# All row scatters beside kernel 1, its softmax sums from a product with ones, and places and owners found by GpSimd in the inverse

## The chip, the cores and the metric

The kernel runs on one core of a Trainium2 chip, in one launch. TensorE (PE) multiplies, VectorE (DVE) and ScalarE (ACT) work on tiles, GpSimd (POOL) does the same and issues indirect DMAs, and SyncE (SP) issues plain DMAs. Each engine runs its own queue of instructions in order; semaphores tie them together. The metric is the device time of the whole launch in microseconds (us), lower being better. Before the change it is 2173.13 us, the median of three runs (2168.01 to 2175.15).

## The reference

Two transformer layers over 4096 rows of 256 numbers, in float32. Only the second concerns us. Its attention is a Nystrom attention (16 heads, 64 landmarks), and beside it stands a mixture of experts, both added to the input:

```python
kernel1 = softmax(einsum('bhnd,bhmd->bhnm', Q, K_l))       # rows against landmarks
kernel2 = softmax(einsum('bhmd,bhkd->bhmk', Q_l, K_l))     # landmarks against landmarks
kernel3 = softmax(einsum('bhmd,bhnd->bhmn', Q_l, K))
for _ in range(6):                                         # iterative_inv(kernel2)
    KV = K @ V
    V = 0.25 * V @ (13 * I - KV @ (15 * I - KV @ (7 * I - KV)))
SV = (kernel1 @ V) @ (kernel3 @ V_rows)
out = SV @ w_proj

scores = sigmoid(x @ router.T)                             # 16 experts, 4 chosen for each row
combine[row, expert] = 2.5 * score / (sum of the 4 chosen)
y = sum_e combine[:, e] * (silu(x @ gate_e.T) * (x @ up_e.T)) @ down_e.T + shared(x)
```

## The kernel before

The second layer runs as a row of stages. Each is an `nc.Block` in which every engine has its own program; the next stage begins when all engines have ended theirs. After kernel 3, whose DVE program also finds the rank of every expert for every row, come the three stages that matter here.

**`inverse` (line 1984).** The six iterations of the inverse for 32 matrices of 64x64, two stacked on the 128 partitions, in four groups `g`. PE computes a step for all four groups (64 pairs of weight load and matmul a step, 21 steps in all), DVE turns each result into the next factor (`polynomial`, `complement`), ACT copies others from PSUM. Beside it the routing is ended. Each row is sent to four slots in HBM, one for each of its four experts; `place[:, k]` holds the slot of a row's choice k, `share[:, k]` its weight, `owner` the expert of each tile of 128 slots. Choice 0 comes from kernel 3. DVE finds the choices 1 to 3 and the owners behind its own work of iterations 0 to 4 (`find_place_and_share`, `compare_owners`, `find_owners`, recorded at line 57 since they go through `Lanes`). SP loads the rows, 4 MB, into `x_rows`. POOL makes small constants and then issues the first 64 (`EARLY`) of 128 scatters: each writes 128 rows of 272 numbers from `x_rows` to their slots. One set of 32 scatters stands for one choice k; before the next set the tag columns of `x_rows` are rewritten, for which the earlier scatters must have landed (lines 2046 to 2057).

**`kernel1` (line 2193).** 32 tiles of 128 rows, in a software pipeline: `staggered(engine, N, DEPTH, [(lag, body), ...])` writes out turns 0 to N + DEPTH, and in turn i each body works on tile i - lag, in the order of the list. For a tile: PE multiplies rows by landmarks (`scores`, into `k_p`), DVE takes the maximum and subtracts it (`shift`), ACT exponentiates (`exp`, `k_e`), DVE sums and takes the reciprocal (`sums`, `k_rs`), POOL multiplies (`normalise`, `k_en`), PE transposes (`turn`, `k_pt`), ACT copies (`take_turned`), PE multiplies by the landmarks' values (`values`, `k_pv`), ACT copies (`take_values`), PE multiplies by w_proj (`output`, `k_po`), DVE adds x1 (`add`, into `QT`). POOL issues two of the remaining 64 scatters ahead of each `normalise`. SP loads the experts' weights first (`load_ahead`) and then the tiles of x1 (`k_x`).

**`experts` (line 2397).** 72 steps of two tiles of slots: load, gate and up, down, and a scatter back to `s_parts`; then the shared experts and the sum. The change does not touch it.

## Time and profile before

| | us |
|---|---|
| median of three runs | 2173.13 |
| the profiled execution | 2178.65 |
| its span in the trace | 2176.2 |
| PE busy in the span | 1814.4 (83%) |
| DVE busy | 1514.0 (70%) |
| ACT busy | 1031.5 (47%) |
| POOL busy | 536.8 (25%) |

The trace covers the span; 2.45 us of the profiled execution lie around it. Busy time is an average over stages with different limits, so the rows further down are read stage by stage. "Idle before" is the idle time of an engine just ahead of an instruction, with what ended it; "issue" stands where the profile shows nothing that was waited for. PE's matmuls and weight loads overlap and have rows of their own (PE and PEld). DMA-issuing instructions of POOL are shown with the time for which they occupy it.

### The profile page before, as it was taken

How to read it: one execution, taken by the hardware profiler on the slowest of the kernel's cores; microseconds unless marked ns; L12 is line 12 of the kernel's file. 1: busy time of each engine (PE TensorE's matmuls, PEld its weight loads, DVE VectorE, ACT ScalarE, POOL GpSimd, SP SyncE). 2: the span in 40 equal slices, each digit the busy share in tenths (PEclk: the TensorE clock that was granted, in tenths of full speed). 3: DMA queues.
4: the chain of work that ended last, by engine and by line, in shares of the span. 5: the costliest groups of instructions: out<-in, count | busy, mean ns of one | idle time of the engine just before them, and what ended most of it. 6: DMA issues, size and time to landing. Idle time of an engine off the chain costs nothing. (4 is left out here: it accounts for less than half of the span.)

```text
span 2176.2 us, 34165 instructions
## 1 busy us (share of the span) xinstructions
PE 1814.4 (83%) x11999; PEld 944.1 (43%) x11999; DVE 1514.0 (70%) x3496; ACT 1031.5 (47%) x1908; POOL 536.8 (25%) x592
## 2 busy tenths in 40 slices
PE   0898926899999999999899959799327788999998
PEld 0565602222222222222223236555317555888865
DVE  7987656888888888888788845378206896444456
ACT  3554403466667666666566825356001444323210
POOL 1443350000000000000340000100650786566620
PEclk9999958999999999999999989999658899999999
DMA  3466563013030404040620163000420622566556
GB/s 97 140 212 220 187 157 69 1 25 127 12 140 3 148 2 150 2 150 2 227 79 11 40 230 128 18 2 1 158 85 9 214 95 94 175 188 187 185 198 222
DMA packets 158712, 238.67 MB, mean 110 GB/s; under 512 B 19762, under 2 KB 127282, under 8 KB 156882
## 3 DMA queue, kind: packets, MB, share of 16 engines
q1 hardware_dynamic: 122706, 152.46, 23.0%
q0 software_dynamic: 23136, 75.65, 9.5%
q10 hardware_dynamic: 12704, 8.39, 1.2%
q8 instruction: 99, 1.62, 0.3%
q14 instruction: 67, 0.55, 0.1%
HBM read 116.23 MB, written 119.82 MB: 108 GB/s over the span
## 5 line engine op out<-in xcount | busy, mean ns | idle before, releaser
L1051 ACT ACTIVATE c_prob<-c_pst 128x512 f32<-128x512 f32 (+1 forms) x1152 | 603.1, 573 | 362.3 <-PE c_pst L1012 221.5
L1159 DVE TENSOR_REDUCE c_mx<-c_pf 128x2 f32<-128x1024 f32 x384 | 463.0, 1223 | 92.3 <-PE c_pf L993 89.4
L1012 PE MATMUL c_pst<-c_qa,c_ka 128*128 128x512 bf16 (+3 forms) x1280 | 393.9, 358 | 38.2 <-DMA c_qa<-c_mT 34.6
L993 PE MATMUL c_pf<-c_ka,c_qa 64*128 64x512 bf16 (+3 forms) x1280 | 234.9, 364 | 79.2 <-DVE c_mx L1159 26.4
L1028 PE MATMUL c_po<-c_prob,c_vh 128*32 128x512 f32 (+3 forms) x2560 | 297.2, 547 | 1.5 <-DVE c_osb L1187 0.5
L1155 DVE CUSTOM_DVE_ANT_0 c_spare<-c_pf,c_cut 128x384 f32<-128x384 f32 (+3 forms) x512 | 231.1, 492 | 51.0 <-PE c_pf L993 46.3
L1012 PEld LDWEIGHTS c_pst<-c_qa,c_ka 128*128 128x128 bf16 x1280 | 108.6, 97 | 284.4 <-ACT c_prob L1051 122.7
L993 PEld LDWEIGHTS c_pf<-c_ka,c_qa 64*128 64x128 bf16 x1280 | 61.9, 93 | 313.0 <-issue 126.5
L925 POOL IOTA c_zero<- 128x24 int32 x6 | 1.3, 215 | 697.4 <-PE c_po L1028 697.4
L1980 POOL DMA_INDIRECT s_parts<-x_yr,x_tags x144 | 141.0, 979 | 85.8 <-DVE x_yr L2635 62.4
L2519 PE MATMUL x_ps<-x_gu,x_xs 128*128 x576 | 137.6, 382 | 0.0
L1980 POOL DMA_INDIRECT s_slots<-x_rows,place x128 | 125.8, 983 | 37.9 <-issue 31.3
L2620 DVE TENSOR_TENSOR x_h<-x_ps,x_sg 128x256 f32<-128x256 f32 x72 | 30.6, 424 | 142.4 <-ACT x_sg L2589 123.5
L2067 PE MATMUL i_pm<-i_X,i_AQ 64*64 64x64 f32 x768 | 41.9, 248 | 82.7 <-issue 70.3
L2519 PEld LDWEIGHTS x_ps<-x_gu,x_xs 128*128 128x128 f32 x576 | 105.0, 192 | 11.5
L1016 PE MATMUL c_pst<-c_negk,c_idb 128*128 128x128 bf16 x512 | 95.7, 220 | 0.0
L1028 PEld LDWEIGHTS c_po<-c_prob,c_vh 128*32 128x32 f32 x2560 | 54.6, 109 | 86.4 <-issue 43.2
L2582 ACT COPY x_xs<-x_ps 128x512 f32<-128x512 f32 x72 | 42.2, 587 | 84.5 <-issue 61.3
L2067 PEld LDWEIGHTS i_pm<-i_X,i_AQ 64*64 64x64 f32 x768 | 35.9, 159 | 88.3 <-issue 75.2
L2540 PE MATMUL x_ps<-x_d,x_hT 128*128 x288 | 74.1, 380 | 0.1
L365 POOL TENSOR_TENSOR b_parts<-b_r,b_parts 128x512 bf16<-128x512 f32 x32 | 57.6, 1819 | 57.7 <-ACT b_parts L502 57.7
L2335 ACT ACTIVATE k_e<-k_d 128x1024 f32<-128x1024 f32 x32 | 33.9, 1060 | 74.0 <-POOL k_en L2271 50.5
(383 smaller groups left out, 2934.9 us busy)
## 6 DMA issues: line engine op xcount, KB each, us to landing
s_slots<-c_zero POOLq DMA_DIRECT2D x6, 3264.0 KB, 19.9
x_xr<-s_slots SPq DMA_DIRECT2D x72, 272.0 KB
x_rows<-s_parts SPq DMA_DIRECT2D x8, 2048.0 KB, 8.8
c_qa<-s_qs SPq DMA_DIRECT2D x64, 192.0 KB, 8.3
c_ka<-s_ks SPq DMA_DIRECT2D x64, 192.0 KB, 9.0
s_qs<-b_parts SPq DMA_DIRECT2D x32, 256.0 KB, 2.4
s_ks<-b_parts SPq DMA_DIRECT2D x32, 256.0 KB, 2.7
s_vs<-b_va SPq DMA_DIRECT2D x32, 256.0 KB, 3.8
```

Source lines behind the costliest of these rows:

```text
L365: nc.gpsimd.tensor_tensor(parts[:, i, 2, :], r[:, i, :], parts[:, i, 1, :], ALU.subtract).then_inc(parts_ok, 1)
L993: mm = nc.tensor.matmul(pf[:, slot, h - fh, 0:kn], qa[r, s, h, qt * P:(qt + 1) * P], ka[r, s, h, k0:k0 + kn], start=True, stop=True, tile_ ...
L1012: mm = nc.tensor.matmul(pst[:, u % NS, at:at + qn], ka[:, s, hh, kt * P:(kt + 1) * P], qa[:, s, hh, qb * QB + q0:qb * QB + q0 + qn], start ...
L1016: mm = nc.tensor.matmul(pst[:, u % NS, at:at + P], idb[:], negk[:], start=False, stop=True)
L1028: mm = nc.tensor.matmul(po[HV * h:HV * h + HV, q0:q0 + qn], vh[:, s, kt, h, :], prob[:, a % NP, h, at:at + qn], start=(kt == 0), stop=(a i ...
L1051: nc.scalar.activation(prob[:, g % NP, hh, 0:w], pst[:, u % NS, 0:w], ACT.Exp).then_inc(exp_ok, 1)
L1155: ins = nc.vector.tensor_tensor_reduce(spare[:, h, 0:kn], pf[:, slot, h, 0:kn], cut[:, W1 - kn:], 1.0, 0.0, ALU.add, ALU.max, mx[:, fh + h ...
L1159: nc.vector.tensor_reduce(mx[:, fh:fh + 2, qt, part], pf[:, slot, :, 0:kn], AX.X, ALU.max).then_inc(max_ok, 1)
L1980: return nc.gpsimd.indirect_dma_start(out=dst, out_offset=bass.IndirectOffsetOnAxis(ap=index.bitcast(U32), axis=0), in_=src, in_offset=None)
L2067: mm = nc.tensor.matmul(out[h, s % 2 * NG + g, k, 0:width], lhs(h, n), rhs(h, n), start=True, stop=True, tile_position=(h.start, h.start))
L2519: mm = nc.tensor.matmul(pgu[:, m % 2, i, :], xs[:, m % 2, i, k, :], gu[:, k, bass.ds(e, 1), :].rearrange("p o n -> p (o n)"), start=(k == ...
L2540: mm = nc.tensor.matmul(pyr[:, m % 2, i, :], hT[:, m % 2, i, :], d[:, bass.ds(e, 1), :].rearrange("p o n -> p (o n)"), start=True, stop=True)
```

## The change

The 64 early scatters leave `inverse`. In their place POOL finds places and shares of the choices 1 to 3 and the owners, in steps that each wait for the one before; a sum over the 16 experts is made by adding halves (8, 4, 2, 1). DVE's program in `inverse` loses that work. POOL waits for the load of `x_rows` at the stage's end.

In `kernel1` POOL issues all 128 scatters, four for each tile, and does nothing else after its constants. `k_e` is transposed as it is, not normalised. PE multiplies the transposed tile not only by the values but also by a matrix of ones (`ones`, block-diagonal, 128x32), which gives each head's sum, repeated on the 16 partitions of that head, beside its values in `k_pv`. DVE takes the reciprocal of these sums (128x256 from PSUM) and multiplies the values by it (`divide`), which replaces `sums` on DVE, `normalise` on POOL and `take_values` on ACT. The pipeline is shorter (DEPTH 6 for 8) and its bodies are ordered anew.

```diff
-            nc.gpsimd.tensor_copy(tiles_f[:], tiles_i[:]).then_inc(consts, 1)
-            nc.gpsimd.memset(xrows[:, :, C:], 0.0).then_inc(tag_ok, 1)
-            pool.wait_ge(tag_ok, 1)
-            for k in range(-(-early // NR)):
-                if k:
-                    pool.wait_ge(sent, 16 * k * NR)
-                nc.gpsimd.iota(xrows[:].bitcast(I32)[:, :, C:C + 1], pattern=[[P * TOPK, NR], [1, 1]], base=k,
-                               channel_multiplier=TOPK).then_inc(tag_ok, 1)
-                wait(pool, share_ok, k)
-                nc.gpsimd.tensor_copy(xrows[:, :, C + 1:C + 2], share[:, k].unsqueeze(2)).then_inc(tag_ok, 1)
-                pool.wait_ge(tag_ok, 2 * k + 3)
-                for t in range(min(NR, early - k * NR)):
-                    if k == 0 and t in (0, NR // 4):
-                        pool.wait_ge(rows_in[t // (NR // 4)], 16)
-                    scatter(nc, slots_dram, place[:, k, t:t + 1], xrows[:, t, :]).then_inc(sent, 16)
-            pool.wait_ge(sent, 16 * early)
+            step(nc.gpsimd.tensor_copy(tiles_f[:], tiles_i[:]))
+            step(nc.gpsimd.memset(xrows[:, :, C:], 0.0))
+            def sum_experts(dst, terms):
+                for n in (8, 4, 2):
+                    step(nc.gpsimd.tensor_tensor(terms[:, :, 0:n], terms[:, :, 0:n], terms[:, :, n:2 * n], ALU.add))
+                step(nc.gpsimd.tensor_tensor(dst, terms[:, :, 0], terms[:, :, 1], ALU.add))
+            def of_choice(dst, val, k):
+                step(nc.gpsimd.tensor_scalar(by[:], rank[:, 0], float(k), None, ALU.is_equal))
+                step(nc.gpsimd.tensor_tensor(by[:], by[:], val, ALU.mult))
+                sum_experts(dst, by)
+            for k in range(1, TOPK):
+                of_choice(placef[:], ahead[:].rearrange("p e t -> p t e"), k)
+                step(nc.gpsimd.tensor_copy(place[:, k], placef[:]))
+                of_choice(share[:, k], comb[:], k)
+            step(nc.gpsimd.tensor_tensor(before[:], ends[0:1, :].unsqueeze(1).to_broadcast([1, NT, E]), over(tiles_f[:], E), ALU.subtract))
+            step(nc.gpsimd.tensor_scalar(before[:], before[:], 0.0, None, ALU.is_le))
+            sum_experts(tiles_f[:], before)
+            step(nc.gpsimd.tensor_scalar(tiles_f[:], tiles_f[:], float(E - 1), None, ALU.min))
+            step(nc.gpsimd.tensor_copy(owner[:], tiles_f[:]))
+            for i in range(2):
+                pool.wait_ge(rows_in[i], 16)
...
-                both(nc.vector.scalar_tensor_tensor, by[:], rank[:, 0], float(k), val, ALU.is_equal, ALU.mult)
-                both(nc.vector.tensor_reduce, dst, by[:], AX.X, ALU.add)
-            def find_place_and_share(k):
-                of_choice(placef[:], ahead[:].rearrange("p e t -> p t e"), k)
-                both(nc.vector.tensor_copy, place[:, k], placef[:])
-                of_choice(share[:, k], comb[:], k)
...
-            def compare_owners():
-                dve.wait_ge(consts, 1)
-                both(tt, before[:], ends[0:1, :].unsqueeze(1).to_broadcast([1, NT, E]), over(tiles_f[:], E), ALU.is_le)
...
-                both(nc.vector.tensor_reduce, ownerf[:], before[:], AX.X, ALU.add)
-                both(ts, ownerf[:], ownerf[:], float(E - 1), None, ALU.min)
-                both(nc.vector.tensor_copy, owner[:], ownerf[:])
...
                 if it < LAST:
                     complement(it + 1)
-                if it + 1 < TOPK:
-                    find_place_and_share(it + 1)
-                elif it + 1 == TOPK:
-                    compare_owners()
-                elif it == TOPK:
-                    find_owners()
...
-    N, DEPTH = B * NT, 8
+    N, DEPTH = B * NT, 6
...
-    en = sb("k_en", [P, 2, H, M])
+    ones = sb("k_ones", [P, 2 * D])
     et = sb("k_et", [P, 2, H // 2, P])
-    mx, sm, rs = (sb(f"k_{n}", [P, 2, H]) for n in ("mx", "sm", "rs"))
+    mx = sb("k_mx", [P, 2, H])
+    rs = sb("k_rs", [P, K, P])
...
-    pv = ps("k_pv", [P, K, P])
+    pv = ps("k_pv", [P, 2, K, P])
...
-            staggered(sp, N, DEPTH, [(6, load)])
+            staggered(sp, N, DEPTH, [(4, load)])
...
+            step(nc.gpsimd.memset(ones[:], 0.0))
+            for h in range(2):
+                step(nc.gpsimd.memset(ones[h * M:(h + 1) * M, h * D:(h + 1) * D], 1.0))
...
-            per = -(-(TOPK * NR - early) // N)
+            per = TOPK * NR // N
 
             def send(n, u, s):
-                for i in range(early + n * per, min(early + n * per + per, TOPK * NR)):
-                    k, t = i // NR, i % NR
-                    if t == 0:
-                        wait(pool, sent, 16 * (i - early))
-                        nc.gpsimd.iota(xrows[:].bitcast(I32)[:, :, C:C + 1], pattern=[[P * TOPK, NR], [1, 1]], base=k,
-                                       channel_multiplier=TOPK).then_inc(tag_ok, 1)
-                        nc.gpsimd.tensor_copy(xrows[:, :, C + 1:C + 2], share[:, k].unsqueeze(2)).then_inc(tag_ok, 1)
-                        pool.wait_ge(tag_ok, 2 * (k - early // NR + (early % NR == 0)))
+                k, t0 = divmod(n * per, NR)
+                if t0 == 0:
+                    wait(pool, sent, 16 * NR * k)
+                    nc.gpsimd.iota(xrows[:].bitcast(I32)[:, :, C:C + 1], pattern=[[P * TOPK, NR], [1, 1]], base=k,
+                                   channel_multiplier=TOPK).then_inc(tag_ok, 1)
+                    nc.gpsimd.tensor_copy(xrows[:, :, C + 1:C + 2], share[:, k].unsqueeze(2)).then_inc(tag_ok, 1)
+                    pool.wait_ge(tag_ok, 2 * (k + 1))
+                for t in range(t0, t0 + per):
                     scatter(nc, slots_dram, place[:, k, t:t + 1], xrows[:, t, :]).then_inc(sent, 16)
 
-            def normalise(n, u, s):
-                wait(pool, r_ok, n + 1)
-                wait(pool, t_ok, n - 1)
-                nc.gpsimd.tensor_tensor(en[:, s], e[:, s], over(rs[:, s], M), ALU.mult).then_inc(n_ok, 1)
-            staggered(pool, N, DEPTH, [(0, send), (3, normalise)])
-            wait(pool, sent, 16 * (TOPK * NR - early))
+            staggered(pool, N, 0, [(0, send)])
+            wait(pool, sent, 16 * TOPK * NR)
 
...
             def turn(n, u, s):
-                wait(pe, n_ok, n + 1)
+                wait(pe, e_ok, n + 1)
 
                 wait(pe, ta_ok, n)
                 for i in range(H // 2):
-                    mm = nc.tensor.transpose(pt[:, i, :], en[:, s, 2 * i:2 * i + 2, :].rearrange("p h m -> p (h m)"), ident[:])
+                    mm = nc.tensor.transpose(pt[:, i, :], e[:, s, 2 * i:2 * i + 2, :].rearrange("p h m -> p (h m)"), ident[:])
...
                 wait(pe, va_ok, n)
                 for k in range(K):
                     for g in range(4):
-                        mm = nc.tensor.matmul(pv[32 * g:32 * g + 32, k, :], W[:, s * (H // 2) + k * 4 + g, :],
-                                              et[:, s, g // 2 * 4 + k * 2 + g % 2, :],
+                        nc.tensor.matmul(pv[32 * g:32 * g + 32, 0, k, :], W[:, s * (H // 2) + k * 4 + g, :],
+                                         et[:, s, g // 2 * 4 + k * 2 + g % 2, :],
+                                         start=True, stop=True, tile_position=(0, 32 * g))
+                    for g in range(4):
+                        mm = nc.tensor.matmul(pv[32 * g:32 * g + 32, 1, k, :], ones[:], et[:, s, g // 2 * 4 + k * 2 + g % 2, :],
                                               start=True, stop=True, tile_position=(0, 32 * g))
                 mm.then_inc(v_ok, 1)
...
-            staggered(pe, N, DEPTH, [(5, turn), (1, scores), (6, output), (5, values)])
+            staggered(pe, N, DEPTH, [(1, scores), (3, turn), (4, output), (3, values)])
...
             def exp(n, u, s):
                 wait(act, d_ok, n + 1)
 
-                wait(act, n_ok, n - 1)
+                wait(act, t_ok, n - 1)
                 nc.scalar.activation(e[:, s], d[:, s], ACT.Exp).then_inc(e_ok, 1)
 
-            def take_values(n, u, s):
-                wait(act, v_ok, n + 1)
-                wait(act, o_ok, n - 1)
-                nc.scalar.copy(svt[:, s], pv[:]).then_inc(va_ok, 1)
-            staggered(act, N, DEPTH, [(5, take_turned), (2, exp), (5, take_values)])
+            staggered(act, N, DEPTH, [(3, take_turned), (2, exp)])
...
-            def sums(n, u, s):
-                wait(dve, e_ok, n + 1)
-                nc.vector.tensor_reduce(sm[:, s], e[:, s], AX.X, ALU.add).then_inc(sum_ok, 1)
-                wait(dve, sum_ok, n + 1)
-                wait(dve, n_ok, n - 1)
-                nc.vector.reciprocal(rs[:, s], sm[:, s]).then_inc(r_ok, 1)
+            def divide(n, u, s):
+                wait(dve, v_ok, n + 1)
+                nc.vector.reciprocal(rs[:], pv[:, 1]).then_inc(rs_ok, 1)
+                wait(dve, rs_ok, n + 1)
+                wait(dve, o_ok, n - 1)
+                nc.vector.tensor_tensor(svt[:, s], pv[:, 0], rs[:], ALU.mult).then_inc(va_ok, 1)
...
-            staggered(dve, N, DEPTH, [(7, add), (2, shift), (3, sums)])
+            staggered(dve, N, DEPTH, [(4, divide), (5, add), (2, shift)])
```

## Rows read from the trace of the kernel before

**Rows 1.** Busy time of each engine (instructions), PEclk, DMA share, GB/s, by stretch.
```profile
1529.30:1541.00 11.70, 8.00 (x252) 7.64 (x252) 5.18 (x13) 1.86 (x5) 7.07 (x15) 1.00 0.90 298
1541.00:1626.00 85.00, 14.81 (x75) 9.88 (x75) 5.44 (x10) 1.12 (x3) 59.16 (x63) 0.52 0.31 114
1626.00:1683.60 57.60, 44.96 (x1017) 44.30 (x1017) 34.13 (x72) 11.51 (x24) 0.00 (x0) 0.85 0.01 2
1683.60:1840.20 156.60, 126.61 (x1152) 86.81 (x1152) 133.78 (x164) 72.76 (x96) 126.55 (x105) 0.93 0.39 132
1840.20:2176.20 336.00, 321.68 (x1552) 255.80 (x1552) 157.56 (x280) 80.79 (x161) 155.51 (x218) 0.98 0.60 192
```
**Rows 2.** Waits, 1529 to 1683: engine and line, releaser: total us, times, longest.
```profile
PE i_pm L2067 <- issue: 73.3, 49, 2.7
PE i_pm L2067 <- DVE i_X L2163: 11.6, 4, 3.4
```
**Rows 3.** Timeline of PE, 1535.9 to 1541.4: start, us, instruction [idle before <-releaser].
```profile
1539.11 1.73 PE L2067 MATMUL i_pm<-i_AQ 64*64 64x64 f32 x52 [2.67 <-issue]
```
**Rows 4.** Timeline of PE, 1619 to 1627.
```profile
1621.37 0.26 PE L2067 MATMUL i_pm<-i_X,i_AQ 64*64 64x64 f32 x1 [2.54 <-issue]
...
1624.88 0.36 PE L2067 MATMUL i_pm<-i_X,i_AQ 64*64 64x64 f32 x1 [0.44 <-issue]
```
**Rows 5.** DMA queues, 1529.3 to 1626: packets, MB, share of 16 engines.
```profile
q8 instruction: 3, 0.05, 0.2%
```
**Rows 6.** Lines, 1541 to 1626: busy us, mean ns | idle before, releaser.
```profile
L1980 POOL DMA_INDIRECT s_slots<-x_rows,place x61 | 59.4, 974 | 18.6 <-issue 18.6
```
**Rows 7.** Timeline of PE, one step of the inverse.
```profile
1670.35 2.08 PE L2067 MATMUL i_pm<-i_X,i_AQ 64*64 64x64 f32 x64
```
**Rows 8.** The page's costliest groups: POOL's operations with two inputs.
```profile
L2271 POOL TENSOR_TENSOR k_en<-k_e,k_rs 128x1024 f32<-128x1024 f32 x32 | 61.1, 1912 | 7.2 <-DVE k_rs L2366 6.6
L365 POOL TENSOR_TENSOR b_parts<-b_r,b_parts 128x512 bf16<-128x512 f32 x32 | 57.6, 1819 | 57.7 <-ACT b_parts L502 57.7
```
**Rows 9.** Timeline of POOL at the change from choice 0 to choice 1.
```profile
1576.19 0.96 POOL L1980 DMA_INDIRECT s_slots<-x_rows,place  x1 [0.31 <-issue]
...
1579.41 1.01 POOL L1980 DMA_INDIRECT s_slots<-x_rows,place  x1 [0.28 <-issue]
```
**Rows 10.** Timeline of DVE, one turn of kernel 1.
```profile
1718.61 0.36 DVE L2373 TENSOR_TENSOR QT<-k_po,k_x 128x256 f32<-128x256 f32 x1
1718.91 1.23 DVE L2354 TENSOR_REDUCE k_mx<-k_p 128x16 f32<-128x1024 f32 x1
1720.17 1.23 DVE L2358 TENSOR_TENSOR k_d<-k_p,k_mx 128x1024 f32<-128x1024 f32 x1
1721.31 1.21 DVE L2362 TENSOR_REDUCE k_sm<-k_e 128x16 f32<-128x1024 f32 x1
```
**Rows 11.** Groups of DVE's instructions by form, whole span.
```profile
L1202 DVE TENSOR_TENSOR c_att<-c_pf,c_rec 128x256 f32<-128x256 f32 x32 | 13.6, 424 | 1.3 <-DVE c_rec L1197 0.3
...
L2366 DVE RECIPROCAL k_rs<-k_sm 128x16 f32<-128x16 f32 x32 | 8.1, 253 | 1.1
...
L1472 DVE RECIPROCAL d_nq<-d_rc 128x4 f32<-128x4 f32 x8 | 1.4, 178 | 0.3
```
**Rows 12.** Timeline of PE, one turn of kernel 1.
```profile
1721.37 0.64 PE L2308 MATMUL k_pv<-k_et,W 128*32 128x128 f32 x16
1721.94 1.09 PE L2299 MATMUL k_pt<-k_ident,k_en 128*128 128x128 f32 x8
1722.97 1.13 PE L2288 MATMUL k_p<-k_kbd,QT 64*128 64x256 f32 x8
1724.03 1.13 PE L2318 MATMUL k_po<-k_wp,k_svt 128*128 128x256 f32 x4
```
**Rows 13.** Timeline of DVE: the first tile's add.
```profile
1714.47 0.42 DVE L2373 TENSOR_TENSOR QT<-k_po,k_x 128x256 f32<-128x256 f32 x1 [7.34 <-DMA k_x<-s_x]
```
**Rows 14.** Lines, 1855.4 to 2086, the experts' scatters.
```profile
L1980 POOL DMA_INDIRECT s_parts<-x_yr,x_tags x144 | 141.0, 979 | 85.8 <-DVE x_yr L2635 62.4 <-issue 23.4
```

More of the change, by code:

```diff
@@ L1981, in scatter, with inverse @@
                                         in_offset=None)
-def inverse(nc, KTb, Vb, VTb, tbd, W, comb, rank, ends, ahead, place, share, owner, rows_dram, xrows, slots_dram, early, TOPK, NPR, ITERS,
+def inverse(nc, KTb, Vb, VTb, tbd, W, comb, rank, ends, ahead, place, share, owner, rows_dram, xrows, TOPK, NPR, ITERS,
             ctx):
@@ L2003, in inverse @@
     C = xrows.shape[2] - 16
-    chain = sem("r_chain2")
     tiles_i = sb("r_tiles_i", [1, NT], I32)
@@ L2009, in inverse @@
     before = sb("r_before", [1, NT, E])
-    ownerf = sb("r_ownerf", [1, NT])
-    consts, share_ok, tag_ok, sent = (sem(f"r_{n}") for n in ("consts2", "share_ok", "tag_ok", "sent"))
     chain_p = sem("r_chain_p")
@@ L2125, in _ @@
             dve.wait_ge(eye_ok, 3)
-            lanes = Lanes(dve, chain, 2)
-            tt, ts = nc.vector.tensor_tensor, nc.vector.tensor_scalar
-            def both(operation, *operands):
-                lanes.join(1)
-                lanes(0, operation, *operands)
-                lanes.last[1] = lanes.last[0]
-            def of_choice(dst, val, k):
-                both(nc.vector.scalar_tensor_tensor, by[:], rank[:, 0], float(k), val, ALU.is_equal, ALU.mult)
-                both(nc.vector.tensor_reduce, dst, by[:], AX.X, ALU.add)
-            def find_place_and_share(k):
-                of_choice(placef[:], ahead[:].rearrange("p e t -> p t e"), k)
-                both(nc.vector.tensor_copy, place[:, k], placef[:])
-                of_choice(share[:, k], comb[:], k)
-                lanes.join(0)
-                dve.sem_inc(share_ok, 1)
-            def compare_owners():
-                dve.wait_ge(consts, 1)
-                both(tt, before[:], ends[0:1, :].unsqueeze(1).to_broadcast([1, NT, E]), over(tiles_f[:], E), ALU.is_le)
-            def find_owners():
-                both(nc.vector.tensor_reduce, ownerf[:], before[:], AX.X, ALU.add)
-                both(ts, ownerf[:], ownerf[:], float(E - 1), None, ALU.min)
-                both(nc.vector.tensor_copy, owner[:], ownerf[:])
-                lanes.join(0)
             def polynomial(s, dst, e, scale):
@@ L2217, in kernel1 @@
     pt = ps("k_pt", [P, H // 2, P])
[L2218 removed]
+    pv = ps("k_pv", [P, 2, K, P])
     po = ps("k_po", [P, 512])
[L2220 to L2221 removed]
+    id0, id_ok, hm_ok, w_in, kbd_ok, chain_p, max_ok, rs_ok = (
+        sem(f"k_{n}") for n in ("id0", "id_ok", "hm_ok", "w_in", "kbd_ok", "chain_p", "max_ok", "rs_ok"))
     tag_ok, sent = sem("k_tag_ok"), sem("k_sent")
     TOPK, NR = place.shape[1], place.shape[2]
[L2224 to L2225 removed]
+    s_ok, d_ok, e_ok, t_ok, ta_ok, v_ok, va_ok, o_ok, x2_ok = (
+        sem(f"k_{n}") for n in ("s_ok", "d_ok", "e_ok", "t_ok", "ta_ok", "v_ok", "va_ok", "o_ok", "x2_ok"))
     x_in = [sem(f"k_x_in{i}") for i in range(2)]
@@ L2718, in two_layers @@
                 owner = layer.enter_context(nc.sbuf_tensor("owner", [1, NSLOT], I32))
-                EARLY = 64
                 with ExitStack() as lm:
@@ L2748, in two_layers @@
                         with ExitStack() as c:
-                            inverse(nc, *stacked, tbd, W, comb, rank, ends, slots_ahead, place, share, owner, rows_dram, xrows, slots, EARLY, TOP_K, NPR, ITERS, c)
+                            inverse(nc, *stacked, tbd, W, comb, rank, ends, slots_ahead, place, share, owner, rows_dram, xrows, TOP_K, NPR, ITERS, c)
                     gu, d, w_in, load = expert_weights(nc, gate_w, up_w, down_w, sh_gate_w, sh_up_w, sh_down_w, C, I, E, NSH, lm)
                     with ExitStack() as c:
-                        kernel1(nc, QT, KS, W, w_proj, x1, load, place, share, xrows, slots, EARLY, B, T, C, M, DA, c)
+                        kernel1(nc, QT, KS, W, w_proj, x1, load, place, share, xrows, slots, B, T, C, M, DA, c)
                     with ExitStack() as c:
```

6 lines of the change are left out of this document (1 added, 5 removed).

## The prediction

> **What bounds the kernel now.** I read the stages around the change first [rows 1]. The inverse (1529.3 to 1683.6, 154.3 us) falls into three parts. In the first 11.7 us PE issues 252 weight-and-matmul pairs. In the next 85.0 us it issues 75, at PEclk 0.52, while POOL issues scatters. In the last 57.6 us it issues 1017. Kernel 1 takes 156.6 us with DVE busy 133.8, PE 126.6 and POOL 126.6; the experts take 336.0 us with PE busy 321.7, and nothing in them is touched.
>
> Next, who waits in the inverse [rows 2]: PE idles 73.3 us on "issue", that is, on nothing that the profile shows, and 11.6 us on DVE's `i_X`. The DVE operations queued ahead of that `i_X` are the places, shares and owners that the change moves away. The timeline shows the "issue" idle to be one event. PE halts at 1536.4, 2.67 us ahead of the row at 1539.11, resumes there with 52 pairs in 1.73 us [rows 3], and then crawls with gaps as long as 2.54 us [rows 4] until it runs freely from 1626 on. From the halt to the free run it issues 52 + 75 = 127 pairs [rows 1, 3], 254 instructions; the queue that carries code moved 3 packets of 16 KB in this time [rows 5]. So the halt looks like a wait for code: it begins while the 4 MB load of `x_rows` holds the DMA engines 90% busy, and the crawl lies over the run of scatters, 1.28 us apart (59.4 + 18.6 us for 61) [rows 6].
> The Trainium skill ("Runtime: NRT & Kernel Launch", Instruction fetch mechanics) says that code comes in blocks of 256 instructions, fetched ahead and mostly hidden. The block size fits the 254; that the fetch is hidden is not what these rows show.
>
> What counts is thus PE's stall in the inverse, and in kernel 1 the longest of three nearly equal loops.
>
> **The inverse.** Removed: 64 scatters. I take the crawl to go with them and the halt to stay, since the `x_rows` load stays. PE has 21 groups of 64 pairs, 1344. After 1541.0, 1344 - 252 = 1092 remain. The last 1017 took 57.6 us, of which 11.6 were the DVE waits [rows 1, 2], hence 46.0; the 75 that crawled cost 75 x 2.08/64 = 2.4 us [rows 7]. The inverse ends at 1541.0 + 46.0 + 2.4 = 1589.4, 94.2 us earlier. Bounds: a new short wait for code adds up to another 2.7 us; less time at half clock takes some 4 away.
>
> Added on POOL: six times an is_equal over 512 elements, a product over 512, adds over 256, 128, 64 and 32, and three casts; then the owners, about 2304 x 2 + 2160 elements on one partition. POOL's two-input operation costs 1.91 us for 1024 elements (1.87 ns each) in one row and 1.82 us for 512 (3.55 ns each) in another [rows 8]. With the first, nearest in type, a choice is 1504 x 1.87 ns = 2.8 us and some 0.8 us of gaps, so 22 us for six, and the owners 6768 x 1.87 ns = 12.7 us and gaps: 36 us, ended near 1569 and covered by PE's stage. With the second it is 39 + 25 = 64 us, ended near 1597, 8 us past PE. I take the first and keep the 8 us.
>
> **Kernel 1, POOL.** Removed: 32 x 1.91 us of `k_en` [rows 8]. Added: 64 scatters. Its queue is now only setup, about 3 us, 128 x 1.28 = 163.8 us, three changes of rank that cost 1.9 us each (1576.19 + 1.28 to 1579.41) [rows 9], and 2 us until the last lands: 175 us. This is a floor under kernel 1 however fast the rest is, 18 us above today's 156.6.
>
> **Kernel 1, DVE.** Removed: the sum of `k_e`, 1.21 us, and the reciprocal of 16, 0.25 us. Kept, from start to start: the add 0.30, the maximum 1.26, the difference 1.14 us [rows 10]. Added: a product 128x256 from PSUM, 0.42 us as `c_att`, and a reciprocal 128x256. No row has that size. From 4 to 16 elements the time rises from 0.178 to 0.253 us, 6.3 ns an element [rows 11], so 256 cost 0.253 + 240 x 0.0063 = 1.76 us; the lower bound is any other 256-wide operation, 0.42 us. I take 1.76, from the rows of the same operation. One turn is 1.76 + 0.42 + 0.30 + 1.26 + 1.14 = 4.9 us, and a few tenths of semaphores: 5.05 us, against the 1.46 + 2.70 = 4.2 us of now.
> The Trainium skill ("VectorE: DVE Perf Modes", First, the fixed hardware budget) describes reciprocal as an iterated divide with a repeat count of 8 at 0.96 GHz; as an estimate from that page 256 elements would be 2.1 us and the turn 5.4. The slope in the rows is lower, and the sum goes by it.
>
> **Kernel 1, PE.** The turned values, transposes, scores and output take 0.57 + 1.03 + 1.06 + 1.13 us from start to start [rows 12]; the 16 passes with ones add about 0.6: 4.4 us, up to 5.0 with today's issue gaps. The transposes need not wait for POOL any more. A chain also closes over both engines: reciprocal and product 2.2, output 1.13, values and ones 1.2, semaphores 0.3, near 4.9. So DVE, PE and the chain stand close to each other, DVE a little ahead.
>
> The first add waits for `k_x`, queued on SP behind the expert weights, until 30.9 us after the stage's start [rows 13]; that queue is unchanged, so the wait stays, and shift and divide are queued behind it on DVE. After it: 2.8 us of that turn, 28 turns x 5.05 = 141.4, and the drain of three short turns, 9.5. Kernel 1 takes 30.9 + 2.8 + 141.4 + 9.5 + 0.4 = 185.0 us, 28.4 more than now; bounds 175 (POOL's floor, if the reciprocal is cheap) and 200 (turn 5.5). ACT loses its copy of the values and idles more, worth nothing.
>
> **Sum.** 2176.2 - 94.2 + 28.4 = 2110.4 us of span, with the 2.45 us around it 2112.9 against the profiled run's 2178.65: 65.8 us less. The median, 2173.13, lies 5.5 below that run, so I forecast 2107.
>
> **Rivals.**
> *The crawl moves into kernel 1.* There 128 scatters now run back to back as in the inverse, the expert weights load over the first 30 us, and PE has 52 pairs a tile where it had 36. If PE runs out of code there once, it pays the same block: 85 us. Against it: kernel 1 and the experts have scatters now (the experts one per 1.6 us [rows 14]) and PE issues freely in both; it needs 104 instructions in 5.05 us, 21 per us; the inverse needed 128 in 2.08 us [rows 7], 62 per us. It decides when code arrives later than one block's 12 us. Price: 2107 + 85 = 2192, slower. Chance 0.10.
> *The crawl is the load's, not the scatters'.* The halt at 1536.4 precedes nearly all scatters; if a late block stays slow whatever POOL does, the inverse keeps its 85 us, loses 11.6 of DVE waits, and kernel 1 still grows by 28.4: 2173.1 - 11.6 + 28.4 = 2190, slower. For it: 254 instructions are as much a block as they are the run of scatters. Against: the crawl's gaps fall from 2.54 us to 0.44 by 1624.88, within 6 us of the last scatters [rows 4], and no other saturated load in the trace brings one. Chance 0.09.
> *POOL is the bound.* Either the reciprocal is cheap, and kernel 1 is 175 us: 2097, inside the forecast; or POOL's vector work is dear and the inverse ends 8 us later: 2115. Both are in the main case.
> *The scatters only shorten the crawl's part.* A second late block, or a partial crawl of 20 to 60 us: 2127 to 2167, faster still or the same. Chance 0.07.
>
> **Chances.** Main case 0.74, own range 2088 to 2135 (bounds of reciprocal, POOL work and code waits: -10, +15, +8, +3 and some slack). Extended by the partial crawls, 2085 to 2150 holds eight in ten. A measurement of this kernel tells about 0.3%, 6.5 us, from no change. Faster: 0.74 and most of 0.07, 0.80; same 0.02; slower 0.18.
>
> **What would show it.** The inverse: PE's "issue" idle falls from 73.3 to under 10 us, PEclk stays near 1, the stage lasts about 60 us. POOL's vector work there sums to 30 to 40 us and ends before PE. Kernel 1: POOL shows 128 scatters 1.28 us apart and nothing else; the reciprocal's mean is 1.7 us; DVE's turn 5.0 us; the stage lasts 175 to 200 us. Wrong would be: long "issue" idle of PE in either stage; a reciprocal near 0.4 us (then POOL ends last); DVE busy under 120 us in kernel 1; or experts that change their 336 us.

## The result, and the profile after

The changed kernel took 2259.93 us (median of 4 runs, 2254.83 to 2268.75) beside 2170.57 us for the kernel before (4 runs, 2167.47 to 2175.15): a ratio of 1.0414, interval 1.0373 to 1.0455. It is slower by 4%; the forecast was 2107 us.

Later runs add a second result. The experiments ran on five chips, and these behaved in two ways. On chips 2 and 13 the kernel before took 2171.4 and 2174.1 us (one run each), as here. On chips 5, 9 and 11 it took 2111 to 2128 us (27 runs). On chip 9 the changed kernel took 2106.89 us (9 runs) beside 2116.33 (18 runs): a ratio of 0.9939, interval 0.992 to 0.9957. I call the first sort of chip "held" and the second "free"; the runs below show why. The held runs all came before the free ones, and no chip was used in both, so whether it is the chip or something at that time isn't shown.

The stages of the changed kernel in its profiled run (2257.39 us, span 2255.7): the inverse, the first kernel, the experts. Columns: stretch, length, busy time and count of PE, PEld, DVE, ACT, POOL, granted clock, DMA share, GB/s.
```profile
1526.80:1585.80 59.00, 48.19 (x1344) 47.04 (x1344) 39.16 (x76) 14.46 (x32) 49.10 (x56) 1.00 0.23 74
1585.80:1920.10 334.30, 152.03 (x1664) 104.20 (x1664) 156.73 (x164) 65.99 (x64) 127.59 (x144) 0.73 0.25 89
1920.10:2255.70 335.60, 321.60 (x1552) 255.77 (x1552) 157.33 (x280) 80.58 (x161) 155.17 (x218) 0.98 0.60 192
```
Against [rows 1], the inverse fell from 154.3 to 59.0 us (60.1 forecast). The experts are unchanged (336.0, 335.6). The first kernel rose from 156.6 to 334.3 us (185.0 forecast). All of the miss, 149 us, is in that stage, where no engine is busy for half of the time.

Who waits there, from the waits of 1585.8 to 1920 (us in total, times, longest):
```profile
ACT k_et L2299 <- remote: 167.3, 2, 99.0
DVE k_rs L2326 <- remote: 165.0, 2, 132.6
...
POOL s_slots L1980 <- issue: 41.0, 125, 3.3
...
PE k_pv L2275 <- issue: 35.7, 2, 34.5
```
ACT and DVE wait 165 us in a few long events on "remote", a releaser that the profile doesn't show; PE waits on "issue". PE's idle on "issue" in the inverse [rows 2, 3] had the same name. The timelines of PE, PEld, DVE and ACT (start, duration, work, idle time before):
```profile
1598.07 1.06 ACT L2305 ACTIVATE k_e<-k_d 128x1024 f32<-128x1024 f32 x1
1667.42 1.01 ACT L2299 COPY k_et<-k_pt 128x1024 f32<-128x1024 f32 x1 [68.29 <-remote]
1668.48 0.66 PE L2275 MATMUL k_pv<-k_et,W 128*32 128x128 f32 x8 [34.54 <-issue]
...
1680.00 0.37 PE L2279 MATMUL k_pv<-k_et,k_ones 128*32 128x128 f32 x1 [2.43 <-issue]
...
1716.40 0.37 PE L2266 MATMUL k_pt<-k_ident,k_e 128*128 128x128 f32 x1 [2.43 <-issue]
1717.80 0.18 PEld L2266 LDWEIGHTS k_pt<-k_ident,k_e 128*128 128x128 f32 x1 [2.62 <-issue]
...
1724.80 0.37 PE L2266 MATMUL k_pt<-k_ident,k_e 128*128 128x128 f32 x1 [2.43 <-issue]
...
1766.82 1.76 DVE L2326 RECIPROCAL k_rs<-k_pv 128x256 f32<-128x256 f32 x1 [132.62 <-remote]
...
1768.37 1.01 ACT L2299 COPY k_et<-k_pt 128x1024 f32<-128x1024 f32 x1 [98.98 <-remote]
```
Two things can be told apart. From 1673 to 1725 PE issues one weight load or matmul each 1.40 us. And DVE and ACT go on long after what they need has been issued: DVE's reciprocal at 1766.8 needs the product whose last matmul started at 1680.0, ACT's copy at 1667.4 the transposes of which the last started at 1605.8, ACT's copy at 1768.4 those of which the last started at 1724.8. PE's long idles follow from this lateness: the one of 34.54 us ends just behind ACT's copy of 1667.4, for which PE's program waits there, although the profile puts it down to "issue". From 1766.8 on the stage runs at a tile in 4.9 us. The scatters on POOL (durations, first and last start):
```profile
L1980 POOL DMA_INDIRECT s_slots<-x_rows,place x128: 956/969/1215, 1588.7 to 1759.4; - x128
```
The stall, which I call the crawl as in the inverse, begins some 12 us after the first scatter and ends 7 us after the last one starts. In the kernel before, the last of the inverse's scatters starts at 1619.0, and its crawl ends at 1626. Crawl and scatters moved together.

### The profile page after: what moved, and what is told of

The parts are those of the page before. It is cut to its first block and busy times, and to the rows that moved or that the text cites. A ratio compares the mean times of both kernels' runs of the same rounds, so it can differ in the third digit from the quotient of the medians.

```text
span 2255.7 us, 35074 instructions
## 1 busy us (share of the span) xinstructions
PE 1821.9 (81%) x12511; PEld 947.3 (42%) x12511; DVE 1530.4 (68%) x3477; ACT 1023.9 (45%) x1876; POOL 519.6 (23%) x610
## 5 line engine op out<-in xcount | busy, mean ns | idle before, releaser
L2326 DVE RECIPROCAL k_rs<-k_pv 128x256 f32<-128x256 f32 x32 | 56.3, 1758 | 169.1 <-remote 165.0
L2584 DVE TENSOR_TENSOR x_h<-x_ps,x_sg 128x256 f32<-128x256 f32 x72 | 30.6, 425 | 142.3 <-ACT x_sg L2553 112.1
L2299 ACT COPY k_et<-k_pt 128x1024 f32<-128x1024 f32 x32 | 32.4, 1012 | 204.8 <-remote 167.3
L2483 PEld LDWEIGHTS x_ps<-x_gu,x_xs 128*128 128x128 f32 x576 | 104.9, 192 | 11.6
L2288 PE MATMUL k_po<-k_wp,k_svt 128*128 128x256 f32 x128 | 38.0, 423 | 84.0 <-DVE QT L2337 58.4
```

The costliest lines, as they stand in the source:

```text
L2326: nc.vector.reciprocal(rs[:], pv[:, 1]).then_inc(rs_ok, 1)
L2483: mm = nc.tensor.matmul(pgu[:, m % 2, i, :], xs[:, m % 2, i, k, :], gu[:, k, bass.ds(e, 1), :].rearrange("p o n -> p (o n)"), start=(k == ...
```

## The experiments

Theory A: a dense run of scatters holds TensorE back. Theory B: a late block of code crawls whatever GpSimd does. Unless said otherwise, edits are to the changed kernel's `kernel1`.

**e1, the scatters last** (chip 2).
```
+            pool.wait_ge(x2_ok, N)
             staggered(pool, N, 0, [(0, send)])
```


> POOL waits until all 32 tiles of kernel 1 are added and only then issues the 128 scatters; all else as in the changed kernel. Theory A (a run of scatters 1.27 us apart holds back what PE sends and receives, for as long as it lasts): PE shows no idle on issue above 2 us in kernel 1; the tiles take 185 us by the prediction's own sum (150 at least), then 166 us of scatters follow, so the whole takes about 2270 us, like the changed kernel, although nothing overlaps. Theory B (a code block that comes late crawls, whatever POOL does): the long issue idle stays somewhere in kernel 1 and the whole takes 2350 us or more.


Measured: 2272.02 us. The tiles are done when the scatters begin at 1761.2, some 178 us after the stage began, and DVE's reciprocal waits 8.5 us in all, none of it "remote":
```profile
L2327 DVE RECIPROCAL k_rs<-k_pv 128x256 f32<-128x256 f32 x32 | 56.2, 1758 | 8.5 <-PE k_pv L2280 8.5
```
The same code without scatters beside it doesn't crawl. Theory B fails for this stage. Doing tiles and scatters in turn costs only 15 us more than doing them together (2257.4), so beside each other they gained almost nothing.

**e2 and e3, at most two or four scatters in flight** (chip 2).
```
+                    done, one = divmod(k * NR + t, 2)
+                    wait(pool, sents[one], 16 * done)
-                    scatter(...).then_inc(sent, 16)
+                    scatter(...).then_inc(sents[one], 16)
```


> At most two scatters in flight (two semaphores in turn, each scatter waits for the last but one). Theory A in the form that it is a backlog of scatters in flight: the backlog cannot form, scatters come 1.3 to 1.5 us apart, PE runs freely, kernel 1 takes 185 to 195 us and the whole about 2105 to 2120 us. Theory A in the form that it is the density: at 1.4 us the stall stays in good part, 2180 us or more. Theory B: no change from 2258 us.

> The same with at most four in flight. If a backlog of more than four forms in the changed kernel, this removes it and gives about 2107 us. If never more than two or three are in flight there (one lands about 2.8 us after its issue), the limit does nothing: 2258 us, and the density alone decides.


Measured: 2210.98 us with two, 2247.45 with four. A limit of four hardly slows the scatters (1585.9 to 1762.3), and the stall stays (ACT's `k_et` waits 122.0 us on "remote"). A limit of two stretches them to 1594.4 to 1800.0, and part of the stall goes. So a backlog of more than four scatters isn't needed for the stall; the distance of the scatters looked like the cause.

**e4 and e7, a gap after each scatter** (chips 2 and 13): the same scatters and waits, with GpSimd kept busy for 0.54 us (a spare block of 128x512) or 0.22 us (128x128).
```
                     scatter(...).then_inc(sent, 16)
+                    step(nc.gpsimd.memset(pad[:], 0.0))
```


> POOL clears a 128x512 tile of its own (0.52 us, and the wait for it) after each scatter, nothing limits what is in flight. Theory A by density: scatters come 1.9 to 2.0 us apart, sparser than the experts' 1.6 us, so PE runs freely; POOL then sets the end, 128 x 1.95 = 250 us, and the whole takes 2106 + 250 - 185 = about 2170 us. Theory B: PE stalls for a block nevertheless, 2250 us.

> The changed kernel with a clear of a spare 128x128 block (by the 128x512 one's 0.54 us an estimated 0.2 us) after each scatter: a scatter every 1.5 us, between 1.42 (two in flight, partial stall, 2211.0 us) and 1.79 (no stall, 2165.3 us). Theory A1, the stall sets in at a sharp rate above 1.5 us: the first kernel is still disturbed, 2190 to 2210 us. Theory A2, it is gone by 1.5 us: scatters done after 128 x 1.5 = 192 us, the whole 2165.3 - 128 x 0.29 = about 2128 us.


Measured: 2165.34 and 2164.99 us, 92 us less than the changed kernel's 2257.39, by slowing GpSimd. The reciprocal's group with 0.54 us, then with 0.22 us:
```profile
L2328 DVE RECIPROCAL k_rs<-k_pv 128x256 f32<-128x256 f32 x32 | 56.3, 1758 | 22.4 <-PE k_pv L2281 22.2
```
```profile
L2328 DVE RECIPROCAL k_rs<-k_pv 128x256 f32<-128x256 f32 x32 | 56.2, 1757 | 74.5 <-remote 67.0 <-PE k_pv L2281 7.6
```
The mean distance of the scatters (from first to last start, over 127) and the "remote" wait of the reciprocal in us: 1.34 us (the changed kernel), 165.0; 1.39 (e3), 82.1 and 63.3 on "issue"; 1.54 (e7), 67.0; 1.62 (e2, uneven), 80.2; 1.87 (e4), none. The mean hides the pattern. In the changed kernel and e3 nearly all scatters are 1.3 us apart, in e7 1.5, in e4 1.8. In e2 most are 1.3 to 1.4 us apart, with pauses of up to 3.6 us between them, which may be why it is held as much as e7 at a larger mean; no run tested that by itself. Neither of my two guesses for e7 (2190 to 2210, or 2128) came true: part of the stall remains, but GpSimd is done 39 us earlier than in e4, and the two cancel. Even in e4 most tiles take 5.38 us, three distances of 1.79, and not 4.9.

**e5, the gap in the kernel before** (chip 13): the same line behind the 64 scatters of its inverse.


> The kernel before with one change: in the inverse GpSimd clears a spare 128x512 block (0.54 us in the run with gaps) after each of its 64 scatters, so that they go out some 1.8 us apart in place of 1.27. Theory A, a dense run of scatters holds TensorE back: the inverse's TensorE runs at its own pace, the stage is then as long as GpSimd needs, 64 x 1.8 = 115 us and some 8 to 12 us around them, 123 to 127 us in place of 154.3, and the whole 2171 - 29 = about 2142 us; no gap of many microseconds without a releaser on TensorE. Theory B, TensorE's late part crawls for a reason of its own: the inverse stays at 154 us and the kernel at 2171 us. The timed result also says whether the crawl that my forecast read as a wait for code was this one.


Measured: 2150.96 us, 23 less than its neighbour of before. The inverse and the first kernel (the inverse really lasts from 1525.7 to 1658.6, so the first stretch leaves out a little at each end):
```profile
1526.80:1656.30 129.50, 56.54 (x1316) 54.68 (x1311) 44.60 (x95) 13.67 (x32) 102.75 (x138) 0.71 0.29 103
1656.30:1812.90 156.60, 127.65 (x1152) 87.62 (x1152) 133.32 (x163) 72.85 (x96) 126.45 (x105) 0.92 0.39 132
```
No wait of PE on "issue" is left among the stage's longest; the largest is 15.2 us on `i_X`. The inverse is now 132.9 us, as long as 64 scatters at 1.8 us and 18 us around them, more than the 8 to 12 that I had put down. The crawl of [rows 2 to 4] was the same one: theory B falls there too.

**e6, small rows** (chip 13): 128 scatters of rows of 64 bytes beside the tiles, the real ones after them.
```
+            for i in range(128):
+                scatter(nc, spare, place[:, i // NR, i % NR:i % NR + 1], small[:]).then_inc(small_sent, 16)
+            wait(pool, small_sent, 16 * 128)
+            pool.wait_ge(x2_ok, N)
             staggered(pool, N, 0, [(0, send)])
```


> The changed kernel with its 128 scatters moved behind the tiles of the first kernel (as in the run with the scatters last, 2272.0 us), and in their old place beside the tiles 128 scatters of rows of 16 numbers (64 bytes) each into a spare table: the same number of instructions and descriptors at the same 1.27 us, one sixteenth or so of the bytes. It does more work than the reference asks for. If it is the bytes that hold TensorE back: tiles at 4.9 us, about 2272 us. If it is the number of instructions or descriptors: TensorE stands as in the changed kernel while they go out (128 x 1.27 = 163 us with almost no tile done), and the whole is about 2272 + 130 to 165 = 2400 to 2437 us. In between: a share of both.


Measured: 2431.27 us, the full stall:
```profile
L2334 DVE RECIPROCAL k_rs<-k_pv 128x256 f32<-128x256 f32 x32 | 56.2, 1757 | 168.9 <-remote 133.3 <-issue 31.6 <-PE k_pv L2287 4.1
```
The same kernel on a free chip (e16) took 2284.65 us, so the stall costs 146.6 us with rows of 64 bytes; with rows of 1 KB it is 149.7 (e14). The bytes don't matter here; what is left is the instructions or their 128 rows each.

**e8, shared and paced** (chip 13): the inverse of the kernel before with 32 of the scatters (and the 128x512 block after each), and in the new first kernel:
```
-            staggered(pool, N, 0, [(0, send)])
+            for i in range(32, TOPK * NR):
+                k, t = divmod(i, NR)
...
+                scatter(nc, slots_dram, place[:, k, t:t + 1], xrows[:, t, :]).then_inc(sent, 16)
+                step(nc.gpsimd.memset(pad[:], 0.0))
```


> The new first kernel, but the inverse of the kernel before (places, shares and owners on VectorE), which sends 32 of the 128 scatters; each of the 128 is followed by the clear of a spare 128x512 block. If density alone was what cost the time: the inverse takes 32 x 1.8 + 8 to 12 = 66 to 70 us, the first kernel 96 x 1.8 = 173 us of GpSimd against 32 turns of 4.9 to 5.3 and some 14 to start, 173 to 184 us; together 239 to 254 against 310.9 before, so 2171 - 57 to 72 = 2099 to 2114 us. If part of the loss comes from elsewhere (VectorE in the inverse, or the scatters' bytes even when paced), 2130 us or more.


Measured: 2136.53 us beside 2174.07. It is faster than both kernels on that chip, though 30 us above the middle of what I expected. The inverse runs from 1524.8 to 1603.3, 78.5 us and not 66 to 70. That isn't the crawl, since the same kernel on a free chip (e18) has 78.8; in both, the last 256 matmuls run at a granted clock of 0.55. The first kernel took 196 us and not 173 to 184; on the free chip it took 187, so some 9 us of it come only on the held chip, where most tiles take 5.4 us and not 4.9.

**e9 to e12** ran on chip 5, where the kernel before took 2118.33 us (7 runs). Their times can't be set against the runs above.

e9, plain transfers in place of the small scatters (`nc.gpsimd.dma_start(spare[i * P:i * P + P], small[:])`, then a 128x384 block):


> The run with small rows (2431.3 us) with one difference: the 128 transfers that GpSimd issues beside the tiles are ordinary ones (128 rows of 64 bytes to fixed addresses), not scatters by an index; a clear of a spare 128x384 block after each keeps them about as far apart (0.54 + 0.42 us and the engine's steps between, an estimated 1.25 us). The real scatters follow the tiles. It writes a spare table that the reference doesn't ask for. If any transfer issued from GpSimd at that rate holds TensorE back: about 2400 to 2430 us. If it takes a scatter by an index: tiles at 4.9 us, as in the run with the scatters last, about 2272 us.


Measured: 2279.62 us, no stall; on this chip that doesn't tell the two kinds of transfer apart, since on chip 11 small scatters cause none either (e16).

e10, the old division: the whole `kernel1` of before, with 128 scatters in it.


> The changed kernel with its second part undone: the first kernel as before (VectorE's row sums, GpSimd's product k_en, one a tile), but with all 128 scatters in it, four a tile; the inverse as in the changed kernel. Theory A, only the rate of the scatters counts: k_en of 1.91 us parts each four scatters from the next four, a tile takes 4 x 1.27 + 1.91 = 7.0 us of GpSimd, the first kernel 14 + 32 x 7.0 = 238 us with TensorE late but never for long, so 2171 - 95 + 81 = 2157 us, up to 2190 if TensorE still stands through each four. Theory C, the run of four is already enough for a full stall: the first kernel as in the changed one, 320 us or more, 2245 us or more. Either way the second part of the change is priced by the distance to 2260 us.


Measured: 2160.86 us. The first kernel:
```profile
1585.80:1823.20 237.40, 149.18 (x1210) 102.29 (x1207) 137.70 (x164) 74.10 (x100) 188.60 (x173) 0.83 0.36 125
```
The stage itself runs from 1588.2 to 1824.4, so 2.4 us of the stretch belong to the inverse: 236.2 us for 238 expected, bound by POOL. The second part of the change is thus worth 51 us beside all scatters on a free chip (184.9 us there, e14). Whether a run of four is already enough for the stall, which this run was to tell, stays open: on a held chip it wasn't run.

e11, places and owners back on VectorE, with the gaps of e4.


> The run with gaps (2165.3 us) with the third part of the change undone: places, shares and owners are found by VectorE between its steps of the inverse, GpSimd has nothing in the inverse but its constants. If TensorE bounds the inverse either way: 59 us and 2165 us, within 3 us. If VectorE's extra work lies on the inverse's chain (its steps wait for each other): the inverse 62 to 70 us, 2168 to 2176 us. If GpSimd's 50 us were what kept the inverse at 59: below 2162 us.


Measured: 2174.93 us. The inverse lasts 72.5 us (1523.2 to 1595.7), against 62.3 in e4 and 59.0 in the changed kernel: the third part is worth 10 to 13 us of the inverse, near the 11.6 us of DVE waits that I took from [rows 2]. The setting differs from e4 in the chip too.

e12, e8 with 24 early scatters in place of 32.


> The shared and paced version (2136.5 us, inverse 75, first kernel 200) with 24 of the scatters in the inverse in place of 32, in three rounds. GpSimd is done with the inverse 8 x 1.79 = 14 us earlier, near 1576, so TensorE ends it near 1590 (63 to 66 us); then 14 us and 32 tiles of 5.4 us, 186 to 190 us, so the experts begin at about 1778 to 1786 and the whole is 2115 to 2123 us, a ratio of 0.974 to 0.978 to the kernel before. If the inverse's TensorE is still held back after the last scatter, 2128 us or more.


Measured: 2142.61 us, ratio 1.0127 (1.0094 to 1.0159): slower by 1.3%. The expected times and ratio took 2171 for the kernel before. Here GpSimd ends last (the tiles are done at 1778, the last scatter starts at 1793.7, and PE's `x_ps` waits 30.6 us for `x_xr`), and a tile beside scatters 1.79 us apart takes 4.87 us, not the 5.38 of e4.

**e13 to e16** put the question to one chip, 11, which proved to be of the free sort.


> The kernel before, unchanged, with its trace. Theory D, chips differ in how far a scatter holds TensorE back: where this takes about 2118 us, the inverse takes some 50 us less than 154.3 (95 to 110 us) and everything else is as it was; where it takes 2171, the inverse is 154 us again. Rival: the 53 us lie elsewhere (the attention or the experts), and the inverse is 154 us on both.

> The changed kernel, unchanged, with its trace. Theory D: on a chip where the kernel before takes 2118 us, the first kernel's scatters hold TensorE back by less, as the inverse's do: if the 64 scatters of the inverse cost some 40 us and not 94, 128 beside tiles cost 80 to 100 of the 165, so 2160 to 2190 us; if they cost next to nothing beside tiles, the forecast's 2107 us. On a chip where the kernel before takes 2171 us: 2255 to 2269 us again.

> The run with plain transfers again (2279.6 us, tiles 4.87 us apart, no stall). If a scatter by an index is what it takes: tiles at 4.9 us on any chip, 2272 to 2282 us. If the earlier run was undisturbed only for its chip, and this one is a chip of the other sort: 2350 us or more.

> The run with small scatters again (2431.3 us, TensorE standing through them), on the same chip as the plain transfers. If the scatter by an index is what it takes: on a chip where the kernel before takes 2171 us, 2425 to 2440 us again; where it takes 2118 us, more than the plain transfers by the share of the stall that chip has, 2300 to 2390 us. If the two kinds of transfer do the same: equal times, within 10 us.


Measured: 2115.92, 2107.71, 2274.02 and 2284.65 us. The kernel before (PE's part of the inverse from 1526.8 on, the rest of it, the first kernel, the experts; the inverse begins at 1521.2 here, so its first 149 matmuls are ahead of the stretch):
```profile
1526.80:1593.20 66.40, 48.51 (x1195) 47.61 (x1191) 41.59 (x87) 12.73 (x27) 48.79 (x50) 0.90 0.40 144
1593.20:1620.60 27.40, 0.04 (x2) 0.00 (x0) 0.00 (x0) 0.27 (x1) 16.00 (x17) 0.52 0.24 88
1620.60:1777.20 156.60, 127.64 (x1152) 87.82 (x1152) 133.76 (x164) 72.60 (x96) 126.72 (x106) 0.93 0.39 132
1777.20:2113.20 336.00, 322.00 (x1552) 255.99 (x1552) 157.58 (x280) 80.71 (x161) 155.26 (x217) 0.98 0.60 192
```
The changed kernel (the inverse, the first kernel, the experts):
```profile
1526.80:1585.80 59.00, 48.41 (x1344) 47.20 (x1344) 39.50 (x76) 14.49 (x32) 49.00 (x56) 1.00 0.22 74
1585.80:1770.20 184.40, 141.62 (x1664) 100.03 (x1664) 156.42 (x163) 66.10 (x64) 128.02 (x144) 0.94 0.47 161
1770.20:2106.00 335.80, 321.22 (x1552) 255.49 (x1552) 157.67 (x281) 80.75 (x161) 155.70 (x218) 0.98 0.60 192
```
Same kernels, scatters as dense as before (in the changed kernel from 1588.9 to 1762.2), and PE isn't held. The kernel before saves 63 us against its first profile: 54 in the inverse, which lasts 100.1 us here (1521.2 to 1621.3) for 154.3, and 8 ahead of it, where the start of the inverse differs by up to 12 us from run to run (1519.5 to 1531.1). The changed kernel saves 150, all in the first kernel. Without the crawl the old inverse is bound by GpSimd's 64 scatters: PE is done at 1593.2, 28 us ahead of the stage's end. The change then takes 41 us from the inverse (100.1 to 59.2) and gives the first kernel 29 (155.6 to 184.9), 12 us less by stages. These two profiles differ by only 7 us of span, since the inverse begins 5.7 us later in the changed kernel's; the nine runs of e17 tell 9 us. Small scatters and plain transfers both leave PE alone here, so e9 and e15 don't tell whether plain transfers stall PE on a held chip. That wasn't tried on one.

**e17 and e18**, on chip 9, of the free sort: the changed kernel (9 runs) and e8's (10 runs).


> The changed kernel, unchanged, in rounds beside the kernel before. On a chip where the kernel before takes 2112 to 2121 us: 2104 to 2112 us, a ratio of 0.994 to 0.999, since both kernels' TensorE runs beside its scatters and what is left is the shift of work itself. On a chip where the kernel before takes 2168 to 2175 us: 2255 to 2269, a ratio of 1.037 to 1.046.

> The shared and paced version (32 scatters in the inverse, 96 in the new first kernel, a clear of 0.54 us after each), unchanged, in rounds. On a chip where the kernel before takes 2168 to 2175 us: 2134 to 2140 us, a ratio of 0.981 to 0.986, faster than both. On a chip where it takes 2112 to 2121 us the pacing buys nothing and costs GpSimd's time: the version with 24 early took 2142.6 us there, with 8 more in the inverse 8 x 1.79 = 14 us less wait at the end, 2126 to 2136 us, a ratio of 1.003 to 1.011.


Measured: 2106.89 us, ratio 0.9939 (0.992 to 0.9957), and 2124.25 us, ratio 1.004 (1.0018 to 1.0061). The changed kernel is faster there, by 0.6%. The paced version is slower there, by 0.4%, and 1.7% faster on a held chip (a single run each of it and of the kernel before). No version was found that beats both kernels on both sorts.

## Why the prediction was wrong

The forecast of 2107 us came true on chips that I hadn't seen, and failed by some 150 us on the one it was made for. The step that failed is the sum for the first kernel: it puts nothing down for PE being held by the scatters that move there. In its place the runs showed 149.9 us, the whole miss. Step by step:

- **The stages.** Wrong in the one that counts: 334.3 us for the first kernel. The reading behind it is in the first paragraphs: the halt and the crawl were taken for one event, a "wait for code", because PE issued 254 instructions from the halt to the free run. They are two things. The halt stands in the changed kernel, with no scatter running:
```profile
1533.50 0.43 PE L2073 MATMUL i_pm<-i_AQ 64*64 64x64 f32 x8
1536.33 1.85 PE L2073 MATMUL i_pm<-i_AQ 64*64 64x64 f32 x56 [2.40 <-issue]
```
  It stands on the free chip too (2.67 us at 1530.95), where no crawl follows. It goes with its place in the program. The crawl goes with the scatters, on some chips. The 254 is then only how far PE had got when the scatters ended, and that it is near 256 is chance. The rule on code blocks that the prediction cites from the Trainium skill ("Runtime: NRT & Kernel Launch", Instruction fetch mechanics) explains neither the 85 us nor the 150: the same code runs through without the crawl in e1, e5 and e14.
- **"I take the crawl to go with them."** It did go from the inverse. What I didn't follow through is that scatters taken out of one dense run were put into a denser and longer one: in the old first kernel each two were parted by `k_en`, 1.91 us [rows 8], and the same change removes `k_en`.
- **The rival had the right place and the wrong price.** "The crawl moves into kernel 1" got 0.10 and 85 us, one block. By rows it should have been the length of the run of scatters: 128 x 1.28 = 164 us, less what PE does in it. Measured: 334.3 - 184.4 = 149.9 us. The evidence that I put against it doesn't hold. PE's need of 21 instructions per us isn't what decides, since the stage is held at that need. It is true that the old first kernel and the experts aren't held: they take 156.6 and 336.0 us on the held chip, 155.6 and 336 on the free one. But their scatters come in pairs, 1.3 us apart, with 3.1 us to the next pair in the old first kernel and 2.0 in the experts. That these pauses are what spares them fits e4, e5 and e7; no run took only the pauses away.
- **The second rival** (the crawl is the load's) is refuted by the changed inverse and by e5.
- **The inverse, 60.1 us:** 59.0. The mechanism is right, with PE's "issue" idle down from 73.3 to 3.2 us. That the number fits to 1.1 us is in part luck: the sum took all 11.6 us of DVE's `i_X` waits away, and 6.7 stay, while the clock is 1.00 where the last stretch of before, from which the sum is taken, had 0.85 [rows 1].
- **POOL's vector work, 36 us with a bound of 64:** 49.1 with the stage's constants, some 46 without, a term sized too low. It is still covered (POOL idles 5.51 us at the end of the stage). The longest rows, by shape:
```profile
L2049 POOL TENSOR_SCALAR r_by<-r_rank 128x512 f32<-128x512 f32 x6 | 9.4, 1562 | 0.5
L2059 POOL TENSOR_SCALAR r_before<-r_before 1x2304 f32<-1x2304 f32 x1 | 6.1, 6090 | 0.1
L2050 POOL TENSOR_TENSOR r_by<-r_by,r_ahead 128x512 f32<-128x512 f32 x3 | 4.6, 1533 | 0.2
L2058 POOL TENSOR_TENSOR r_before<-r_ends,r_tiles_f 1x2304 f32<-1x2304 f32 x1 | 4.3, 4284 | 0.1
```
  That is 1.86 to 3.05 ns an element, where I had taken 1.87. The short adds cost more still: 741 ns for 256 elements and 353 ns for 64, that is 2.9 and 5.5 ns an element, so no price per element fits all of them.
- **The reciprocal of 256, 1.76 us by the slope of [rows 11]:** 1.758. The estimate from the Trainium skill ("VectorE: DVE Perf Modes", First, the fixed hardware budget), 2.1 us, is not borne out; the rows of the same operation at other sizes were the better source.
- **The turn, 5.05 us, and the first kernel, 185.0:** 4.87 and 184.4, where PE isn't held. On the free chip, two turns of DVE's reciprocal:
```profile
1702.06 1.76 DVE L2326 RECIPROCAL k_rs<-k_pv 128x256 f32<-128x256 f32 x1
1706.94 1.76 DVE L2326 RECIPROCAL k_rs<-k_pv 128x256 f32<-128x256 f32 x1
```
  The sum was sound as a model of a stage in which PE isn't held, though two of its terms partly cancel: the first add comes at 33.4 us and not 30.9, and 28 turns are 5 us shorter. That the whole, 2106.89 us, meets the forecast of 2107 is right for these stages and still not what was forecast: the gain there is 9 us and not 66, since the baseline loses the crawl as well and becomes bound by GpSimd.
- **The chances.** 0.80 for faster rested on one cause being gone. A stall whose releaser the profile doesn't name had to carry more than 0.10 for returning wherever its companion goes.

**Open.** What sets the two sorts of chip apart, and whether it is the chip or something at the time: all runs of the kernel before on the free chips lie within 2111 and 2128 us, and those on the held ones within 2167 and 2179. Through what the scatters reach PE, DVE and ACT: the stall doesn't follow the bytes (e6), and it stays with at most four in flight (e3). Whether plain transfers from GpSimd do it on a held chip. Whether a short run of dense scatters is enough. And where it sets in: at a steady 1.3 us the stall is full, at 1.5 it is partial, at 1.8 only the slower tile is left.

## What to carry to other kernels

When an engine idles on "issue" or "remote" for as long as another engine runs one kind of instruction, count it as likely that the idle follows that instruction: price every place that the change moves it to by the length of the run there, and look at what parts those instructions today, since the change may remove it. Before trusting a cause read off a coincidence, vary the companion's rate: one cleared block behind each scatter (e4, e5) separated the theories and gained 92 us. And time the baseline on more than one chip and at more than one time; this change saves 9 us on one sort and costs 89 on the other.

## What the runs showed of the hardware

- In the changed kernel's profile, and likewise on chips 2 (e3) and 13 (e6), scatters by an index from GpSimd some 1.28 us apart stop PE almost entirely from some 12 us after the first to the last. DVE and ACT go on late: DVE 87 us after PE's last matmul of `k_pv` had started, ACT 62 and 44 us after the last transpose of `k_pt`. 64-byte rows do it as 1 KB rows do (e6). On chips 9 and 11 the same kernels show none of it, nor do the kernels run on chip 5.
- PE's granted clock falls with the idle: in the changed kernel's profile it is 0.73 over the first kernel, and 0.51 from 1619 to 1777, next to the lower of its two levels (1.2 of 2.4 GHz), while PE was busy for 20.3 of 158 us; on a free chip it is 0.94 over the first kernel.
- A clear of a 128x512 block on GpSimd takes 0.54 us, of 128x128 0.22 us; a scatter of 128 rows occupies GpSimd for 0.96 us with rows of 64 bytes and for 0.97 with rows of 1 KB (medians of 128), a plain transfer of 128 rows of 64 bytes for 0.54 us.
